# Row statistics of the first quarter by two passes on ScalarE, transposes in two pairs of banks, and a reordered drain of the convolution

## What is computed

```python
h = conv1d(x, conv_in_w, stride=1, pad=3)
h = gelu(groupnorm1(h, gn1_w, gn1_b))
h = conv1d(h, dw_w, stride=2, pad=2, groups=H) + dw_b[None, :, None]
h = conv1d(h, pw_w)
h = gelu(groupnorm1(h, gn2_w, gn2_b))
...
h = h + attn(layernorm(h), Wq, Wk, Wv, Wo)
...
def layernorm(x, axis=-1, eps=1e-05):
    m = mean(x); v = var(x)
    return (x - m) / sqrt(v + eps)
```

## Time and profile before

| | us |
|---|---|
| median of 3 runs | 2828.05 |
| lowest, highest | 2826.13, 2829.7 |
| the profiled execution, its own time | 2826.87 |
| its span in the trace, first to last instruction | 2825.1 |

### The profile page before, as it was taken

The page is one execution under the profiler, slowest core; times in us unless marked ns, Lnnn a source line. Parts: engine busy times, 40 slices in busy tenths (PEclk is TensorE's granted clock), DMA queues, the critical chain, the costliest instruction groups (busy, mean ns, idle before and its releaser), DMA issues. The chain is left out here.

```text
span 2825.1 us, 37124 instructions
## 1 busy us (share of the span) xinstructions
PE 2709.9 (96%) x13162; PEld 2240.3 (79%) x13162; DVE 1806.2 (64%) x3217; ACT 979.0 (35%) x2012; POOL 107.8 (4%) x65
## 2 busy tenths in 40 slices
PE   7996999999899999999999999899999988899999
PEld 5664788888788888887888888788888876688888
DVE  4888766666766666677666666776665665862221
ACT  3554333333433333334333333333333333542121
POOL 2110000000000000000000000000000000221110
PEclk9997999999999999999999999999999999999999
DMA  5320322223222222222222222222222224000000
GB/s 128 74 60 21 109 79 78 82 74 97 63 91 94 82 82 75 81 82 68 81 77 83 95 89 82 75 75 82 82 74 82 75 66 157 1 23 23 30 22 31
DMA packets 55327, 206.69 MB, mean 73 GB/s; under 512 B 6769, under 2 KB 7153, under 8 KB 53169
## 3 DMA queue, kind: packets, MB, share of 16 engines
q1 hardware_dynamic: 55216, 205.26, 23.0%
HBM read 196.85 MB, written 8.39 MB: 73 GB/s over the span
## 5 line engine op out<-in xcount | busy, mean ns | idle before, releaser
L801 PE MATMUL at_proj<-qr_xhi,at_whi 128*128 128x512 f32 x1536 | 617.8, 402 | 6.4 <-DVE qr_xlo L220 4.4
L803 PE MATMUL at_proj<-qr_xhi,at_wlo 128*128 128x512 f32 x1536 | 602.4, 392 | 0.0
L802 PE MATMUL at_proj<-qr_xlo,at_whi 128*128 128x512 f32 x1536 | 601.0, 391 | 0.0
L960 ACT CAST at_ohi<-at_ov 128x512 fp32r<-128x512 f32 x128 | 75.0, 586 | 847.2 <-PE at_ov L1204 847.2
L801 PEld LDWEIGHTS at_proj<-qr_xhi,at_whi 128*128 128x128 f32 x1536 | 290.4, 189 | 64.0 <-issue 4.1
L803 PEld LDWEIGHTS at_proj<-qr_xhi,at_wlo 128*128 128x128 f32 x1536 | 289.8, 189 | 63.9
L802 PEld LDWEIGHTS at_proj<-qr_xlo,at_whi 128*128 128x128 f32 x1536 | 290.8, 189 | 57.2 <-issue 0.5
L1222 PE MATMUL at_out<-at_wohi,at_ohi 128*128 128x512 f32 x1008 | 311.2, 390 | 4.0 <-DVE at_wolo L1070 3.0
L1222 PE MATMUL at_out<-at_wohi,at_olo 128*128 128x512 f32 x1008 | 310.9, 390 | 0.0
L1222 PE MATMUL at_out<-at_wolo,at_ohi 128*128 128x512 f32 x1008 | 310.7, 389 | 0.0
L1077 DVE TENSOR_TENSOR h<-h,at_out 128x1024 f32 (+1 forms) x126 | 152.8, 1213 | 210.9 <-PE at_out L1222 210.9
(11 more groups left out here) (259 smaller groups left out, 3973.6 us busy)
## 6 DMA issues: line engine op xcount, KB each, us to landing
at_wstage<-in_w_qkv_dram SPq DMA_DIRECT2D x192, 512.0 KB, 3.7
at_ostage<-in_w_o_dram SPq DMA_DIRECT2D x128, 512.0 KB, 4.5
cv_x<-in_x_dram SPq DMA_DIRECT2D x32, 512.0 KB, 6.5
out_dram<-h SPq DMA_DIRECT2D x16, 512.0 KB, 2.6
fn_w_lo_raw<-in_w_t_dram SPq DMA_DIRECT2D x8, 512.0 KB, 9.8
fn_qka_lo_raw<-in_qka_t_dram SPq DMA_DIRECT2D x5, 512.0 KB, 12.0
fn_w_lo_raw<-in_dft_fwd_dram SPq DMA_DIRECT2D x4, 512.0 KB, 7.2
shared_raw<-in_a_route_dram SPq DMA_DIRECT2D x1, 544.0 KB, 4.2
```

The source lines that it names most:

```text
L801: pe.matmul(proj[:, j % 2, :], hi[:, w], x_hi[:, k, :], start=(k == 0), stop=False)
L802: pe.matmul(proj[:, j % 2, :], hi[:, w], x_lo[:, k, :], start=False, stop=False)
L803: last = pe.matmul(proj[:, j % 2, :], lo[:, w], x_hi[:, k, :], start=False, stop=(k == KT - 1))
```

## The change

Four things are edited, all in the convolution's last two full iterations and its drain.

1. The statistics of the first quarter's rows leave VectorE. ScalarE takes, for each of the four batches, a sum over the row (`sums`: an Identity pass over `h` with an accumulator), then the negative mean, then the sum of squares around it (`squares`: a Square pass with the negative mean as bias and an accumulator). The passes write the buffers `xn`, whose contents are overwritten later. Batches 0 and 1 stand in iteration 14, batches 2 and 3 in iteration 15: the sums at the iteration's start, the squares between its two evacuations. VectorE makes the coefficients from the results (`first_coefficients`, thirteen linked instructions) between its `middle` and its last taps in iteration 15.
2. `turn`, `high` and `low` take a number of bank pairs, `sets`; the first quarter uses two pairs of the four banks `cp`, so that a turn waits for `low` of two batches ahead.
3. The drain is reordered on all three engines. On TensorE the averages of iteration 16 move behind project 0 and project 1, and pointwise 14 behind both; averages of 17 stand around project 2. On VectorE the low halves move ahead of the statistics of batch 15, the taps and the middle; weights' low halves move up. On ScalarE the splits of weights and the high halves move up.
4. Three tiles of 128x4 and a semaphore are added.

```diff
+        self.total, self.minus, self.around = (sb(n, [P, QB]) for n in ("total", "minus", "around"))
...
+    def sums(self, act, *batches):
+
+        if batches[0]:
+            act.wait_ge(self.moments, batches[0] // 2 * 5)
+        for b in batches:
+            act.activation(self.xn[b % 2][:, :], row(self.h, b), ACT.Identity, accum_out=self.total[:, b:b + 1])\
+               .then_inc(self.moments, 1)
+        first, n = batches[0], batches[0] // 2 * 5 + 2
+        act.wait_ge(self.moments, n)
+        these = slice(first, first + 2)
+        act.activation(self.minus[:, these], self.total[:, these], ACT.Identity, scale=-1.0 / L)\
+           .then_inc(self.moments, 1)
+
+    def squares(self, act, *batches):
+
+        act.wait_ge(self.moments, batches[0] // 2 * 5 + 3)
+        for b in batches:
+            act.activation(self.xn[b % 2][:, :], row(self.h, b), ACT.Square, bias=self.minus[:, b:b + 1],
+                           accum_out=self.around[:, b:b + 1]).then_inc(self.moments, 1)
+
+    def first_coefficients(self, dve):
+
+        link = Links(dve, self.norm, 1)
+        dve.wait_ge(self.moments, self.MOMENTS)
+        link(dve.tensor_scalar(self.var[:, :], self.around[:, :], 1.0 / L, EPS, ALU.mult, ALU.add))
+        rsqrt(dve, self.rstd[:, :], self.var[:, :], self.tmp[:, :], link)
+        dve.tensor_tensor(self.shift[:, :], self.minus[:, :], self.rstd[:, :], ALU.mult)\
+           .then_inc(self.norm, self.LINKS - link.n)
...
-    def turn(self, pe, qt, banks, *batches):
+    def turn(self, pe, qt, banks, *batches, sets=1):
...
-                if b > 0:
-                    after(pe, self.lo_done, qt * self.UNITS + 2 * b + c - 1)
+                if b >= sets:
+                    after(pe, self.lo_done, qt * self.UNITS + 2 * (b - sets) + c + 1)
...
-                    last = pe.transpose(banks[:, c, k * P:(k + 1) * P], self.xn[b % 2][:, at:at + P],
+                    last = pe.transpose(banks[:, b % sets * 2 + c, k * P:(k + 1) * P], self.xn[b % 2][:, at:at + P],
...
+                    if from_end(it) == 6:
+                        act.wait_ge(gelu2, QB)
+                        rows.sums(act, 0, 1)
+                    if from_end(it) == 5:
+                        rows.sums(act, 2, 3)
                     if from_end(it) == 4:
-                        act.wait_ge(xlo_done, NB)
-                        pro.split_w(act, 0, 0)
-                        rows.high(act, 0, cp, 0)
+                        pro.split_w(act, 0, 1)
+                        rows.high(act, 0, cp, 0, sets=2)
                         rows.normalize(act, 0, 2)
+                        rows.high(act, 0, cp, 1, sets=2)
...
+                    if from_end(it) == 4:
+                        rows.normalize(act, 0, 3)
+                        rows.high(act, 0, cp, 2, sets=2)
+                        rows.high(act, 0, cp, 3, sets=2)
...
                         evacuate(it, par, 0)
+                        if from_end(it) == 6:
+                            rows.squares(act, 0, 1)
+                        if from_end(it) == 5:
+                            rows.squares(act, 2, 3)
                         evacuate(it, par, 1)
                     if from_end(it) == 5:
+                        act.wait_ge(xlo_done, NB)
+                        pro.split_w(act, 0, 0)
                         rows.normalize(act, 0, 0)
                         rows.normalize(act, 0, 1)
...
+                    if from_end(it) == 5:
+                        rows.first_coefficients(dve)
                     if on(2):
                         taps(it - 2, par, (3, 4))
-                    if from_end(it) == 5:
-                        dve.wait_ge(gelu2, QB)
-                        link = Links(dve, rows.norm, 1)
-                        for b in range(QB):
-                            rows.stats(dve, 0, link, b)
-                        rows.coefficients(dve, link)
-                        rows.keep(dve, link, rows.rstd[:, :], rows.shift[:, :])
...
                     def last_16():
                         tail(15)
-                        heads(16, 0, on, lambda: rows.low(dve, 0, cp, 0))
+                        rows.low(dve, 0, cp, 0, sets=2)
+                        rows.low(dve, 0, cp, 1, sets=2)
                         dve.wait_ge(conv_done, NB * NCH)
                         pro.low_w(dve, 0, 0)
+                        head(1, 13, [pp[:, c, :] for c in range(2)])
+                        rows.low(dve, 0, cp, 2, sets=2)
+                        rows.low(dve, 0, cp, 3, sets=2)
+                        head(0, 15, [raw[1][:, c // 2, c % 2 * BANK:(c % 2 + 1) * BANK] for c in range(NCH)])
+                        pro.low_w(dve, 0, 1)
                         taps(14, 0, (1, 2))
-                        rows.low(dve, 0, cp, 1)
                         middle(16)
-                        rows.low(dve, 0, cp, 2)
-                        rows.low(dve, 0, cp, 3)
                         taps(14, 0, (3, 4))
-                        pro.low_w(dve, 0, 1)

                     def last_17():
                         tail(16)
                         dve.wait_ge(pro.rope_in, 16)
                         pro.rope_out(dve, 0, 0, 0)
+                        pro.low_w(dve, 0, 2)
                         heads(17, 1, on, lambda: None)
                         taps(15, 1, (1, 2))
-                        pro.low_w(dve, 0, 2)
                         middle(17)
-                        taps(15, 1, (3, 4))
                         pro.rope_out(dve, 0, 0, 1)
                         pro.low_w(dve, 0, 3)
+                        taps(15, 1, (3, 4))
...
                     def last_16():
                         pe.wait_ge(raw_done, NB * 2)
-                        rows.turn(pe, 0, cp, 0, 1)
+                        rows.turn(pe, 0, cp, 0, 1, 2, sets=2)
                         pointwise(13, 1)
+                        rows.turn(pe, 0, cp, 3, sets=2)
+                        pro.project(pe, 0, 0, 0)
                         average(16, on, 0)
-                        rows.turn(pe, 0, cp, 2)
+                        pro.project(pe, 0, 0, 1)
                         average(16, on, 1)
-                        rows.turn(pe, 0, cp, 3)
-                        pro.project(pe, 0, 0, 0)

                     def last_17():
                         pointwise(14, 0)
-                        pro.project(pe, 0, 0, 1)
                         average(17, on, 0)
+                        pro.project(pe, 0, 0, 2)
                         average(17, on, 1)
-                        pro.project(pe, 0, 0, 2)
```

More of the change, by code:

```diff
@@ L160, in __init__ @@
         self.dummy = sb("dummy", [P, 1])
+        self.total, self.minus, self.around = (sb(n, [P, QB]) for n in ("total", "minus", "around"))
+        self.moments = sem("moments")
         self.norm = sem("norm")
@@ L185, in keep @@
         assert link.n == self.LINKS
+    MOMENTS = 2 * QB + QB // 2
+    def sums(self, act, *batches):
[21 more added lines that the diff above has]
+           .then_inc(self.norm, self.LINKS - link.n)
     def normalize(self, act, qt, b):
@@ L199, in turn, with high @@
             for c in range(2):
-                if b > 0:
-                    after(pe, self.lo_done, qt * self.UNITS + 2 * b + c - 1)
+                if b >= sets:
+                    after(pe, self.lo_done, qt * self.UNITS + 2 * (b - sets) + c + 1)
                 for k in range(KT // 2):
                     at = (c * KT // 2 + k) * P
-                    last = pe.transpose(banks[:, c, k * P:(k + 1) * P], self.xn[b % 2][:, at:at + P],
+                    last = pe.transpose(banks[:, b % sets * 2 + c, k * P:(k + 1) * P], self.xn[b % 2][:, at:at + P],
                                         self.ident[:, :])
                 last.then_inc(self.turned, 1)
-    def high(self, act, qt, banks, b):
+    def high(self, act, qt, banks, b, sets=1):
         for c in range(2):
@@ L212, in high, with low @@
             act.copy(self.x_hi[:, c * KT // 2:(c + 1) * KT // 2, b * P:(b + 1) * P],
-                     banks[:, c, :].rearrange("p (k t) -> p k t", t=P)).then_inc(self.hi_done, 1)
-    def low(self, dve, qt, banks, b):
+                     banks[:, b % sets * 2 + c, :].rearrange("p (k t) -> p k t", t=P)).then_inc(self.hi_done, 1)
+    def low(self, dve, qt, banks, b, sets=1):
         for c in range(2):
@@ L219, in low @@
             tiles, cols = slice(c * KT // 2, (c + 1) * KT // 2), slice(b * P, (b + 1) * P)
-            dve.tensor_tensor(self.x_lo[:, tiles, cols], banks[:, c, :].rearrange("p (k t) -> p k t", t=P),
-                              self.x_hi[:, tiles, cols].bitcast(F32), ALU.subtract).then_inc(self.lo_done, 1)
+            dve.tensor_tensor(self.x_lo[:, tiles, cols],
+                              banks[:, b % sets * 2 + c, :].rearrange("p (k t) -> p k t", t=P), self.x_hi[:, tiles, cols].bitcast(F32), ALU.subtract).then_inc(self.lo_done, 1)
 def conv_stage(nc, h, ident, ones_mean, x, conv_w, dw_w, chan, pw_wT, rope, rows, w_stage, pro):
```

(3 more changed lines are left out.)

## The result

| | before | after |
|---|---|---|
| median of 4 runs each, us | 2827.09 | 2845.99 |
| lowest, highest | 2825.76, 2829.7 | 2839.65, 2847.09 |
| span of the profiled execution | 2825.1 | 2837.9 |

The ratio is 1.0064, with a 95% interval from 1.0051 to 1.0077: **slower by 0.64%**, and outside the predicted range. The profiled execution of after is the quickest of its four (2839.65), so its span shows 12.8 of the 18.9 us that separate the medians.

A forecast was written before the change was run, and what follows sets the result against it. VectorE was taken to come closest to bounding the drain: 228.2 + 64.3 work + 8.4 waits = 300.9 against 309.65, 8.7 us less, so 2818.2 from the profiled execution, 2819 as median; range 2813 to 2826.

The forecast's parts named there:

- Rival D: Attention stage: three new tiles move all its buffers; matmuls slowed by 0.7% (14 us) would give 2833 us; chance 0.04.
- The drain's term: VectorE's queue in the drain: start 228.2, work 64.3, waits 8.4, end 300.9 against 309.65; 8.7 us less, between 13.7 and 3.7.
- wait 3: VectorE in the drain: middle 16 waits for average 16, now behind project 0 on TensorE; 2.2 us (0 to 4.5).
- wait 2: VectorE in the drain: head 13 waits for pointwise 13, itself behind Gelu 12; 1.7 us at half clock, 0.5 at full.
- Wait 4: VectorE in the drain: tail 16 waits for the second average, now behind project 1 on TensorE; 2.5 us (to 5).
- wait 6: Late drain, VectorE behind TensorE: middle 18 waits 0.6 and tail 18 0.7 us for an average's round trip; 1.3 in the sum.
- ScalarE's passes: Convolution's last two full iterations: eight added passes of 1.2 us each fit ScalarE's idle time; 0 in the sum, 0.5 at most.
- Norms and turns: Drain's start: coefficients ready at 230.9 instead of 240.25, first transposes at 232.5 instead of 241.68, project 0 at 246.4 instead of 263.94.
- The new stall for Gelu 13: TensorE in the drain, ahead of pointwise 14: idle from 260.5 to 265.1, as Gelu 13 needs tail 16; about 4.7 us.
- A: The drain gets no shorter: the reorder hands back what the statistics freed, waits 13.5 to 17, time 2823 to 2827; chance 0.14.
- B: Slower: TensorE's clock stays low through the drain, its queue ends at 325.5, time 2843 us; chance 0.05.
- C: ScalarE's Square needs another table: two loads in the path, 2.6 us, time 2821.5; chance 0.04.

## Why the prediction was wrong

**The step that failed** is the first: nothing that the change touches runs behind 312 us, "so that part can only move as a block". The change's code doesn't run there, but its tiles moved the operands of the 4464 projection matmuls there, and the part became 27.7 us longer. Rival D named this, "the moved tiles", and had it wrong twice: its chance was 0.04 because "no row shows such a dependence", and its price was 14 us where the stage grew by 27.7. Its sign came as described: behind the drain the lengths were no longer those of before. A trace of one layout can't show what another layout costs, so the lack of a row was no evidence. What could have raised the chance stood in the code: a tile that nothing reads, 96 bytes long, just behind the rows' halves, which makes the distance to the weights exactly 97 x 512, and a change that adds 96 bytes to it.

**The drain's term** was under-sized. By the prediction's own mark, the end of VectorE's last weight half, it was 8.7 us forecast and 14.6 measured (309.65 to 295.08), past its upper bound of 13.7. Of that, 1.4 is a drain that merely began earlier; its start lies between 226.3 and 228.1 in versions of before, so this part is scatter. The other 13.2 are inside the bounds. By the sum: it starts at 226.8 in place of 228.2, VectorE's work is 63.6 in place of 64.3, the waits 4.7 in place of 8.4; 226.8 + 63.6 + 4.7 = 295.1 against 300.9. The waits were the mis-sized term. Project 0 started at 243.7 in place of 246.4 and went at the full clock from its first matmul, 5.7 us to the average at 249.41, where half clock at first had been taken from before. So wait 3 (2.2 forecast; its start of 246.4 and 7.9 us make 254.3 and not 254.5) vanished, and wait 2 was 1.0 for 1.7. Wait 4 was 2.3 for 2.5, wait 6 1.1 for 1.3 on VectorE's side.

**Point by point, the rest of the steps.**
- Statistics off VectorE: thirteen linked instructions from 226.83 to 229.44, 2.6 as forecast.
- ScalarE's passes: 1.05 between the starts of the sums, 1.14 for the squares, below the 1.2 taken; the read of the accumulator (0.18 to 0.19) overlaps with the next pass. The squares fit, the last evacuation starts at 226.75.
- Norms and turns: the first transposes at 230.9, forecast 232.5.
- The new stall for Gelu 13 ahead of pointwise 14: 4.39, forecast 4.7, with half clock in the pointwise behind it (3.43), and average 17's wait 1.04 for 1.4.
- A didn't happen. B didn't: the drain's mean clock rose from 0.77 to 0.90; behind project 0 only pointwise 14 ran at half clock, after the stall. C didn't: between Gelu and Square stands no table load, in any of the four squares (the loads nearest to them start at 38.87 and 297.76 us). By the list of functions in the Trainium skill (ScalarE: Activation LUTs, section Table sets: the hidden batching unit), which doesn't name Square, C had been left possible; this trace decides against it.

With the operands where they had been, the forecast holds: 2819.07 measured, 2819 forecast. That agreement is partly luck, since the drain alone gave more.

## What to carry to other kernels

A new tile is part of a change's cost even if it is 16 bytes long: list what is allocated behind it, and keep the distance between the operands that TensorE streams and loads where it was, or test the layout by itself (the kernel before with only the tile made larger is such a test). A tile that nothing uses may be there for the layout; ask what it lines up before adding to it. When a stage that nobody edited changes its length, compare mean times per instruction form first: one row, 391 against 397 ns at equal counts, pointed to the loss here, and the times from start to start gave its size. And check that an edit to a layout moves what it is meant to move: tiles take whole multiples of 32 bytes, so padding that is worked out from a tile's own length can leave the distance as it was.

## What the runs showed of the hardware

In the projections, dense runs of 128x512 matmuls that each load their own weights, the pace depends on where tiles lie relative to the rows that TensorE streams: 0.227 us where the distance to the weights is a multiple of 256 bytes, 0.233 to 0.234 at 32, 64, 96 and 128 bytes off (medians of the last twelve steps of all projections), at the same granted clock of the stage (0.99 before and after) and with the same recorded load of weights (188 to 190 ns). That is 3% on these matmuls, and 1% of this kernel. Why is open: the records show longer spacing, not what it waits for.

The Trainium skill (SBUF — State Buffer, section Who interferes with whom) gives TensorE two independent read ports, one for the moving operand and one for loads of weights, and says that "PE and ACT never wait on anyone." No run here shows whether TensorE waited for another engine, so that sentence stands untested. But independent ports don't foretell a pace that changes with addresses, and the measurement has one: 0.227 against 0.233 to 0.234 us with the same instructions.

The output products, at 389 to 392 ns in all versions, moved by the same bytes as the weights, but both of their operands lie behind the moved tiles, so that their distance never changed; it is a multiple of 512 bytes, and their pace is 0.227.
